# The half-size value fill moves from place 2 to place 3 of a round, and the context's rows are rounded in five pieces instead of four

## The reference

```
q = split_heads(layernorm(x) @ Wq.T + bq)          # 16 heads of 16
k = split_heads(ctx @ Wk.T + bk)                   # 1601 keys a batch
v = split_heads(ctx @ Wv.T + bv)
x = x + softmax(q / 4 @ k.T) @ v  -> heads joined -> @ Wo.T + bo
```

## Time and profile before

| | us |
|---|---|
| three runs | 2097.88, 2099.88, 2231.48 |
| median | 2099.88 |
| the profiled execution's own time | 2097.24 |
| its span, from the first to the last instruction | 2095.2 |
| granted TensorE clock, mean of the span | 0.984 |

### The profile page before, as it was taken

One profiled execution on the slowest core, in us unless ns is written; L12 is line 12 of the kernel. 1 busy time (PEld: TensorE's weight loads), 2 busy tenths in 40 slices (PEclk: granted clock), 3 DMA queues, 4 the chain that ended last, 5 costly groups with the idle time before them and its releaser, 6 DMA issues.

```text
span 2095.2 us, 72878 instructions
## 1 busy us (share of the span) xinstructions
PE 1967.4 (94%) x31836; PEld 1589.1 (76%) x31852; DVE 1289.2 (62%) x2276; ACT 1048.9 (50%) x1532; POOL 675.5 (32%) x1349
## 2 busy tenths in 40 slices
PE   6889999999999999999999999999999999999987
PEld 5677777887878887787878778787787777777764
DVE  2556656756656566766666585665666676565644
ACT  3345445555465555456555544555544444444441
POOL 4323333423233333333424233442324232123201
PEclk7999999999999999999999999999999999999999
DMA  5533434343433343434333425243342422222122
GB/s 183 179 126 105 161 119 136 124 138 116 136 119 115 106 145 118 133 117 145 125 118 124 146 78 166 88 156 102 110 150 86 121 71 66 75 71 89 50 72 71
DMA packets 124473, 243.92 MB, mean 116 GB/s; under 512 B 13953, under 2 KB 44801, under 8 KB 124161
## 3 DMA queue, kind: packets, MB, share of 16 engines
q1 hardware_dynamic: 123568, 239.23, 34.9%
q10 hardware_dynamic: 592, 0.04, 0.0%
HBM read 235.94 MB, written 3.15 MB: 114 GB/s over the span
## 4 chain that ended last, share of the span: by engine, by line
PE 77%; DVE 8%; ACT 7%; issue 5%; POOL 2%; DMA 0%; SPq 0%; POOLq 0%; DVEq 0%; ACTq 0%
PE M L818 12%; PE M L825 11%; PE SC L1037 10%; PE SC L1060 8%; PE O L1081 8%; PE X L875 5%; ACT probT L1281 4%; PE SC L1053 3%; DVE mx L1630 3%; PE M L875 3%; PE X L1147 2%; PE M L920 1%; PE M L880 1%; PE X L854 1%; PE X L1121 1%
## 5 line engine op out<-in xcount | busy, mean ns | idle before, releaser
L1630 DVE TENSOR_REDUCE mx<-SC 128x4 f32<-128x1600 f32 (+1 forms) x256 | 466.9, 1824 | 158.1 <-PE SC L1037 154.8
L1281 ACT ACTIVATE probT<-SC 128x2048 f32<-128x2048 f32 (+1 forms) x256 | 398.8, 1558 | 157.1 <-PE SC L1060 156.6
L658 POOL TENSOR_TENSOR rowsT<-raw,rowsT 128x256 fp32r<-128x256 f32 (+1 forms) x512 | 326.8, 669 | 365.1 <-ACT rowsT L1335 365.0
L825 PE MATMUL M<-wvs,rowsT 128*128 128x256 f32 x2496 | 357.5, 292 | 3.1 <-ACT kT L1222 1.4
L818 PE MATMUL M<-rowsT,wks 128*128 128x400 f32 (+1 forms) x1536 | 341.9, 363 | 5.9 <-POOL rowsT L658 1.2
L1222 ACT ACTIVATE kT<-M,bk 128x400 f32<-128x400 f32 (+1 forms) x256 | 151.4, 593 | 376.8 <-PE M L818 376.2
L818 PEld LDWEIGHTS M<-rowsT,wks 128*128 128x128 f32 x1536 | 271.8, 191 | 79.5 <-issue 63.7
L825 PEld LDWEIGHTS M<-wvs,rowsT 128*128 128x128 f32 x2496 | 313.6, 191 | 23.8 <-issue 2.6
L1426 DVE TENSOR_TENSOR V<-M,bv 128x512 f32<-128x512 f32 (+1 forms) x224 | 145.3, 649 | 255.8 <-PE M L825 250.6
L1037 PE MATMUL SC<-kT,bdq 32*128 32x400 f32 (+1 forms) x2048 | 248.3, 550 | 27.3 <-ACT probT L1281 23.4
L1081 PEld LDWEIGHTS O<-probT,V 128*17 128x17 f32 x13312 | 195.0, 100 | 68.5 <-issue 64.0
(11 more groups left out here) (283 smaller groups left out, 2445.3 us busy)
## 6 DMA issues: line engine op xcount, KB each, us to landing
ring<-in_ws_dram SPq DMA_DIRECT2D x428, 256.0 KB, 4.3
summed<-in_ctx_dram SPq DMA_DIRECT2D x60, 800.5 KB, 4.7
raw<-in_ctx_dram SPq DMA_DIRECT2D x64, 384.0 KB, 4.0
raw<-in_ctx_dram SPq DMA_DIRECT2D x32, 512.0 KB, 4.2
ring<-rounded_scratch SPq DMA_DIRECT2D x64, 256.0 KB, 3.8
raw<-in_ctx_dram SPq DMA_DIRECT2D x32, 321.0 KB, 4.8
out_dram<-x SPq DMA_DIRECT2D x16, 128.0 KB, 1.7
kT<-in_ctx_dram SPq DMA_DIRECT2D x2, 800.5 KB, 8.7
```

The lines of the kernel that those rows point to most:

```text
L658: ins = pool.tensor_tensor(rowsT[1][:, c, part], raw[:, c, part], rowsT[0][:, c, part], ALU.subtract)
L825: mm = pe.matmul(bank[:, (t - 2 * a) * D:(t - 2 * a + 1) * D], rowsT[xp][:, cc, t * P:(t + 1) * P], wvs[wp][:, cc, :], start=(at == cc == ...
L1281: act.activation(probT[step % 3][0:w, :, 0:len(ts), :].rearrange("p j t q -> p j (t q)"), SC[0:w, :, 0:len(ts) * P], ACT.Exp)\
L1630: dve.tensor_reduce(mx[c][:, :, n], SC[:, :, 0:KCH[n][1]], AX.X, ALU.max).then_inc(max_used, 1)
```

## The change

In `FIRST`, `value(6)` and `value(0)` exchange places: `value(0)`, of two tiles, is filled in place 2 and `value(6)`, of one tile, in place 3. The last piece of rows (tiles 10 to 12) is divided: tiles 10 and 11 keep the place of rounding (high part in place 2, low part in place 3), and wait for the fill of `value(5)`; tile 12 is a piece of its own, with its high part in place 3 and its low part in place 4, and waits for `value(6)`. Its load is issued in place 6. A piece of one tile has one low instruction for each half of the features instead of two. `len(PIECES)` enters the counts for which the fills wait.

```diff
-FIRST = [[[value(4)], [value(5)], [value(6)], [value(0)], [key(0, 3)], [value(1)], [value(3)], [value(2)]],
-         [[value(4)], [value(5)], [value(6)], [value(0)], [key(0, 3)], [value(1)], [value(3)], [value(2)]]]
+FIRST = [[[value(4)], [value(5)], [value(0)], [value(6)], [key(0, 3)], [value(1)], [value(3)], [value(2)]],
+         [[value(4)], [value(5)], [value(0)], [value(6)], [key(0, 3)], [value(1)], [value(3)], [value(2)]]]
 SECOND = [[[key(0, 0)], [key(0, 1)], [], [key(0, 2)], [key(1, 0)], [key(1, 1)], [], [key(1, 2), key(1, 3)]],
           [[], [key(0, 0), key(0, 1)], [], [key(0, 2)], [], [key(1, 0), key(1, 1)], [], [key(1, 2), key(1, 3)]]]
...
-FIRST_SPLITS = (-24, -24, -19, -18), (-18, -18, -16, -13)
+FIRST_SPLITS = (-24, -24, -19, -18, -18), (-18, -18, -16, -13, -13)
...
-LOAD_AT = (1, 2, 3, 5)
-
-PIECES = [(0, 4, key(1, 1)), (4, 7, key(1, 2)), (7, 10, value(4)), (10, KT, value(VF - 1))]
+LOAD_AT = (1, 2, 3, 5, 6)
+
+PIECES = [(0, 4, key(1, 1)), (4, 7, key(1, 2)), (7, 10, value(4)), (10, KF, value(5)), (KF, KT, value(VF - 1))]
...
-    for piece, at in enumerate((-2, -1, 0, 2)):
+    for piece, at in enumerate((-2, -1, 0, 2, 3)):
...
-                        for part in (slice(lo * P, mid * P), slice(mid * P, hi * P)):
+                        for part in (slice(lo * P, mid * P), slice(mid * P, hi * P)) if hi - lo > 1 else (at,):
                             ins = pool.tensor_tensor(rowsT[1][:, c, part], raw[:, c, part], rowsT[0][:, c, part], ALU.subtract)
```

## The result

| | before | changed kernel |
|---|---|---|
| median of six runs, us | 2098.82 | 2124.06 |
| lowest and highest, us | 2091.39, 2231.48 | 2117.88, 2140.29 |
| profiled execution: its time, its span, us | 2097.24, 2095.2 | 2117.88, 2116.0 |

The ratio is 1.0147, with a 95% interval of 1.0114 to 1.0180: slower by 1.5%, within the 2% of "no change", as forecast (2128 us, 1.3% over the 2099.88 it started from). The execution of 2231.48 us was a slow one and is left out of the ratio. The medians of the table are 25 us, or 1.2%, apart, so 1.2 to 1.5% is what these executions tell. The profiled execution of the changed kernel is the shortest of its six, and it ran at a granted clock of 0.988 where that of before had 0.984, so its 20.8 us understate the difference. PE's idle time grew by 25.9 us (span less busy time: 2095.2 - 1967.4 and 2116.0 - 1962.3).

The account below looks back on a forecast made before the run. TensorE was taken to bound the kernel. A wait of 38 us, less 3.7 for the exchange and 5 given back, plus 1 for the prologue, made some +30 us: 2128 us forecast, range 2102 to 2144.

Parts of the forecast that it names:

- The wait: In place 4, key(0, 3) waits for tile 12's low part: 38 us, at least 19, up to 10 more.
- the rounds that were named: Place 4 waits told by round: 0.25 us in 10, 18, 24; 1.9 in 4, 14, 16; 3.9 in 20.
- plain odd rounds: Twelve odd rounds whose drain of `ff0` ends 0.73 us before key(0, 3) in place 4: 0.9 us of wait each.
- the rule of the Trainium skill: GpSimd shares SBUF interfaces with VectorE; alone it puts place 4's odd-round low parts at their floor, 4 us less.
- The exchange: Swapping value(6) and value(0) between places 2 and 3 gives back 9.5 - 5.8 = 3.7 us.
- The place 2 half: The larger value fill covers idle time before place 2's maxima: 9.5 us gone over rounds 1 to 30.
- The place 3 half: The smaller value fill in place 3 turns slack behind the exponential into new waits: 5.8 us over the rounds.
- Given back: Other engines catch up while PE stands, shrinking idle time in places 4 to 7: 5 us, between 2 and 15.
- The prologue: Before the rounds, a DMA, a ScalarE instruction and two of GpSimd are added: under 1 us, counted as 1.
- A: Rival: place 4's wait comes but is mostly given back, places 5 to 7 shrink; 2105 to 2115 us; chance 0.22.
- B: Rival: places 2 and 3's swap outweighs a wait under 0.12 us a round; 2090 to 2096 us; chance 0.05.
- C: Rival: GpSimd's wait at place 4's head delays deviations and softmax; from +42 us, priced +44, 2144 us; chance 0.10.

Follow-up runs that it names:

- experiment 1: Changed kernel with the exchange of value(6) and value(0) undone, tile 12's rounding still a place late: 2123.26 us, ratio 1.0145 to the kernel before.
- experiment 2: Kernel before with only the last piece divided, tile 12 its own piece in the same places as tiles 10 and 11: 2095.95 us, ratio 1.0001.
- experiment 3: Changed kernel with tile 12's rounding moved forward within place 3 on both ScalarE and GpSimd: 2092.52 us, ratio 0.9992 to the kernel before.
- experiment 5: Changed kernel with only ScalarE's high part of tile 12 moved forward, ahead of place 3's second drains: 2115.09 us, ratio 1.0086 to the kernel before.
- experiment 6: Changed kernel with only GpSimd's low part of tile 12 moved forward into place 3: 2112.47 us, ratio 1.0067 to the kernel before.
- experiment 7: Changed kernel with tile 12's rounding moved forward on both engines and value(6) back in place 2: 2097.31 us, ratio 1.0006 to the kernel before.
- experiment 4: Changed kernel with four pieces, all of tiles 10 to 12 rounded a place late, in places 3 and 4: 2198.49 us, ratio 1.0510 to the kernel before.
- experiment 9: Changed kernel with four pieces, the whole last one rounded in place 3, high part ahead of the second drains: 2090.65 us, ratio 0.9980 to the kernel before.

## Why the prediction was right

**The wait.** Forecast 38 us, measured 31.8 in 27 waits, in the rounds that were named: nothing in 1, 10, 18 and 24; 2.99 in rounds 8 and 22 (2.7 said), 3.65 in 20 (3.9), 2.10 in 13 (2.3), 1.74 to 1.79 in 4, 14 and 16 (1.9). The plain odd rounds were off in size, 0.60 for 0.9 us in eleven of them; the odd rounds together waited 10.5 us for the 14.4 forecast. Two low parts took 0.87 us, not 1.03, and the high part (0.41 us, 0.43 said) began 0.1 us before the drain ahead of it had ended. The 0.87 us are two low parts at the floor of the earlier trace rows; I kept the mean and should have taken the floor. That floor is what the rule of the Trainium skill ("GPSIMD Engine Reference", Specifications) let one expect where VectorE works from PSUM. The trace agrees, but it doesn't single the rule out: in round 20, with no VectorE instruction beside them, two low parts took 0.86 us. Experiments 1 to 3 show that this wait, with the clock behind it, is the whole loss, 5 and 6 that it has two causes.

**The exchange.** Forecast -3.7 us: 9.5 us of idle time gone from place 2, 5.8 new in place 3. Measured in the profiles, over the same rounds 1 to 30: 10.0 gone and 10.2 new (with round 0, 11.6 and 11.1). The place 2 half was right. The place 3 half was little more than half of what came, because it was reckoned from the slack behind the exponential alone, which came to 2.7 us of new waits there, and left out VectorE: L1089 waits 4.4 us more in place 3, L944 2.9 us. The other 7.2 of the 7.7 us by which the two places shrank are PE's busy time. Rounds 0, 3, 19 and 27 hold 5.3 of the 7.7; the other 27 rounds give 2.4. Place 2 of round 27, before and after:

```profile
1773.30:1783.28 9.98, 8.72 (x197) 6.93 (x195) 7.55 (x17) 3.27 (x4) 4.93 (x11) 0.83 0.09 28
```

```profile
1794.01:1802.64 8.63, 7.86 (x203) 6.65 (x201) 7.19 (x17) 3.06 (x4) 3.65 (x10) 1.00 0.12 32
```

and place 3 of round 3:

```profile
293.29:304.43 11.14, 8.32 (x59) 6.68 (x60) 7.23 (x8) 2.81 (x6) 7.49 (x13) 0.85 0.41 150
```

```profile
289.07:298.59 9.52, 5.97 (x53) 4.43 (x54) 7.06 (x8) 2.81 (x6) 5.61 (x11) 1.00 0.45 165
```

Round 27 is no accident of one execution. Its place 2 has a clock of 0.70 to 0.83 in the four profiles with `value(6)` there (before, experiments 1, 2 and 7) and 1.00 in the seven with `value(0)` there; in round 0 it is 0.73 in the four and 0.87 to 0.91 in the seven. Place 3 of round 3 is low in some profiles of either order. So what the exchange gives seems to come through the clock in a few places more than through the waits, which I had not foreseen. In round 27, PE's longest stop in place 2, ahead of L1139, went from 1.03 to 0.57 us; that this keeps the clock up is not shown. No pair of times shows it: experiment 1, without the exchange, and the changed kernel have 1.0145 and 1.0147 (their spans are 5.4 us apart), and experiments 7 and 3 overlap. So the times don't show even the sign of this term.

**Given back.** This term was wrong in kind. I took 5 us off, since the others catch up while PE stands. Place 4 itself gave back 2.0 us (the wait grew by 30.6, the idle time of place 4 by 28.6), which is the lower end that I named; places 5 and 6 gave back nothing. And the stops cost beyond their length, by the clock. In the changed kernel that was 4.4 us (the busy time of place 4; rounds 8 and 13). In experiment 4 it was about a quarter of the loss: 21.5 us more busy time of the 98.0 us between its span and that of before, or 26.6 of 77.2 against the changed kernel.

**The prologue.** Forecast +1 us; the first scores came at 89.6 us instead of 91.2, where the clock differed too (windows of 0 to 89.62 and 0 to 91.2 us: 0.89 and 0.85). No cost seen, but 1 us would be hidden by the clock.

**The rivals.** A (mostly given back) falls: place 4 grew by 33.0 us for a wait that grew by 30.6, and places 5 and 6 gave nothing back. B (not slower) falls with experiment 1, but experiments 3 and 9 are B's condition made true. C (GpSimd a second bound): in the changed kernel its waits don't spread; in experiment 6, where VectorE does wait longer for the deviations, PE hardly feels it. The forecast of some +30 us on the profiled execution met +20.8 (+25 by the medians). In the sum, errors cancelled: the wait was 6 us too long, 3 of the 5 us weren't given back, and neither the 4 us of low clock in place 4 nor the 7 us by which PE's busy time fell in places 2 and 3 was in it. So the wait, which makes the loss, was forecast rightly; that the total came so near is in part luck.

## What to carry to other kernels

When a producer's step is moved by one place, write down what is queued ahead of it on each of its engines at the new point, and where its first reader stands; a place's nominal distance says nothing if one step sits at the end of its place and the next at the head of another's queue. Here 0.73 us of cover stood against 1.3 us of rounding, and the mend was to move the step within the place. An exchange that saves a tenth of a microsecond a round is worth making only after its followers are checked, those on every engine, for here the new stops on the bound engine were hardly given back.

## What the runs showed of the hardware

- A stop of TensorE can cost more than its length. In some of the places with stops of 1.8 to 5.0 us the granted clock fell to means of 0.70 to 0.88, in others, as in round 20 of the changed kernel with 3.65 us, it stayed at 1.00, as it did there with all the stops of 0.5 to 1.8 us. The same stop (3.65 us, round 20) left it at 1.00 in the changed kernel and brought it to 0.85 in experiment 1. Which of the long stops bring it down stays open, and it fell in places 4 without such a stop too (round 18: 0.84 in experiment 2, 0.77 in 3). Filling the stops with 310 useless matmuls took the places 4 with a low clock from 18 to none, raised the mean clock from 0.974 to 0.990 and saved 28.6 us of 2198.5.
- Two profiled executions of nearly the same program can differ by 6 us and more of PE busy time (1961.1 in experiment 3, 1967.7 in 9) through short spells of lower clock. Spans of single profiles are not fit to judge 0.3%; waits and sums by place are, once the places with a lower clock are set apart.
- The four shapes of the high part lie near one line: 256 columns 410 ns, 512 623, 768 846, 1024 1051, that is 0.20 us and 0.83 ns a column.
